# Routed mixture-of-experts layer: second products in half precision, the normalisation split over two engines, and a deep ring of sorted rows

## What is computed

```python
xn = layernorm(x)
# attention part: one gathered number for each token, then a broadcast product
off = xn @ W_off + b_off; w = softmax(xn @ W_attn + b_attn)
s = sum(take(xn[:, 0, :], int(off[..., 0])) * w)
attn = broadcast(s) @ W_out + b_out
# two shared experts, all tokens; eight routed experts, two of them for each token
ffn(x, w1, w2, w3) = silu(x @ w1.T) * (x @ w3.T) @ w2.T     # 128 -> 256 -> 128
shared = sum(ffn(xn, sw1[i], sw2[i], sw3[i]) for i in range(2))
rw, sel = top_k(xn @ router_w.T + expert_bias, 2); rw = softmax(rw)
out = x + attn + shared + sum(rw[k] * ffn(xn, expert sel[k]) for k in range(2))
```

## Time and profile before

| what | us |
|---|---|
| median of 3 runs | 528.65 |
| lowest and highest | 527.91, 529.05 |
| the profiled execution, its time | 530.35 |
| its span, first to last instruction | 528.4 |
| TensorE busy in the span | 453.4 (86%) |
| VectorE busy | 336.8 (64%) |
| ScalarE busy | 219.6 (42%) |
| GpSimd busy | 241.7 (46%) |

### The profile page before, as it was taken

How to read it: one execution, slowest core, us unless ns; L and a number is a source line. 1 busy time by engine, 2 the same in 40 slices (tenths; PEclk the granted TensorE clock), 3 DMA queues, 4 the chain that set the end, 5 groups by cost and what they waited for, 6 DMA issues and landing times.

```text
span 528.4 us, 15190 instructions
## 1 busy us (share of the span) xinstructions
PE 453.4 (86%) x5200; PEld 382.1 (72%) x5200; DVE 336.8 (64%) x973; ACT 219.6 (42%) x399; POOL 241.7 (46%) x225
## 2 busy tenths in 40 slices
PE   0166676787999999999989999999999999999990
PEld 0155533454667777777779999899998999989990
DVE  4899799989676999999756664333333333333330
ACT  1255741172124555554424444344444444443430
POOL 0134400246745333432000001888888887656563
PEclk9999898899999999999989999999999999999997
DMA  8999400000411111111122332445454444232000
GB/s 242 263 156 167 65 1 1 10 26 27 144 53 37 48 51 48 45 45 40 30 89 97 113 103 77 56 53 65 50 67 48 61 57 56 37 52 37 3 3 0
DMA packets 50684, 34.61 MB, mean 65 GB/s; under 512 B 9408, under 2 KB 44224, under 8 KB 50624
## 3 DMA queue, kind: packets, MB, share of 16 engines
q1 hardware_dynamic: 32048, 23.88, 19.9%
q0 software_dynamic: 15296, 8.53, 12.4%
q10 hardware_dynamic: 3280, 1.36, 1.1%
HBM read 14.87 MB, written 20.69 MB: 67 GB/s over the span
## 4 chain that ended last, share of the span: by engine, by line
PE 70%; DVE 18%; issue 3%; DMA 3%; ACT 2%; ACTq 2%; another core or an unknown queue 1%; POOL 0%; DVEq 0%; POOLq 0%
PE pY L611 17%; PE pAB L591 11%; PE pAB L593 8%; PE pAB L592 8%; PE pY L463 7%; DVE units L889 5%; PE pAB L448 4%; PE pAB L450 4%; PE pAB L449 4%; PE pV L488 3%; PE pV L475 3%; PE pV L574 2%; DVE hbuf L913 2%; ACTq L625 2%; DMA base<-in_x 1%
## 5 line engine op out<-in xcount | busy, mean ns | idle before, releaser
L796 POOL DMA_INDIRECT out_dram<-hot,meta x92 | 142.7, 1551 | 62.2 <-DMA out_dram<-base 18.2
L1157 DVE SCALAR_TENSOR_TENSOR hbuf<-pAB,units 128x512 f32<-128x512 f32 x92 | 63.7, 692 | 120.3 <-PE pAB L593 109.1
L591 PE MATMUL pAB<-xT,wsp 128*128 128x128 f16 x736 | 138.2, 220 | 1.7 <-issue 0.8
L593 PE MATMUL pAB<-xT,wsp 128*128 128x128 f16 x736 | 138.4, 220 | 0.0
L592 PE MATMUL pAB<-xT,wsp 128*128 128x128 f16 x736 | 138.2, 220 | 0.0
L777 POOL DMA_INDIRECT sorted_rows<-rows,slot x64 | 70.1, 1096 | 112.7 <-DVE hbuf L913 56.9
L611 PE MATMUL pY<-wsp,hbuf 128*128 x736 | 104.1, 284 | 2.9 <-issue 2.7
L735 ACT ACTIVATE units<-pAB 128x512 f32<-128x512 f32 x92 | 54.9, 597 | 119.8 <-PE pAB L593 117.6
L611 PEld LDWEIGHTS pY<-wsp,hbuf 128*128 128x128 f32 x736 | 89.8, 191 | 5.5 <-issue 3.3
L689 ACT ACTIVATE units<-pAB 128x512 f32<-128x512 f32 x64 | 38.0, 597 | 114.5 <-PE pAB L450 101.3
L591 PEld LDWEIGHTS pAB<-xT,wsp 128*128 x736 | 71.0, 96 | 13.9 <-issue 3.3
(11 more groups left out here) (136 smaller groups left out, 566.0 us busy)
## 6 DMA issues: line engine op xcount, KB each, us to landing
sorted_rows<-c_pad_row SPq DMA_DIRECT2D x1, 6026.0 KB, 46.7
wraw<-sorted_rows SPq DMA_DIRECT2D x46, 131.0 KB
base<-in_x SPq DMA_DIRECT2D x4, 1024.0 KB, 8.2
out_dram<-base SPq DMA_DIRECT2D x16, 256.0 KB, 2.5
wraw<-in_wall SPq DMA_DIRECT2D x8, 256.0 KB
out_dram<-hot,meta POOLq DMA_INDIRECT x92
sorted_rows<-rows,slot POOLq DMA_INDIRECT x64
wsp<-in_wall SPq DMA_DIRECT2D x8, 128.0 KB
```

Of the source, the lines that this page charges most:

```text
L591: pe.matmul(o, hi, x(0), start=True, stop=False)
L593: mm = pe.matmul(o, lo, x(0), start=False, stop=True)
L796: pool.indirect_dma_start(out_rows, bass.IndirectOffsetOnAxis(ap=meta[:, t % Y_RING, DEST - CW:DEST - CW + 1].bitcast(U32), axis=0), yt[:, ...
L1157: v.scalar_tensor_tensor(hbuf[:, r % 4, :], pAB[:, 2 * (r % 2) + 1, :], 1 / (XS * WS), silu[:, r % 2, :], ALU.mult, ALU.mult).then_inc(d_h ...
```

## The change

1. *Front.* ScalarE normalises three of the four tiles of a block (`activation` with scale and bias) and VectorE the fourth; the fp16 high half moves from ScalarE to VectorE. Statistics and scales come in three parts of 4, 4 and 8 blocks instead of two of 8.
2. *Routed second products.* `w2` is split into fp16 halves like `w1` and `w3` (768 columns of each routed expert instead of 512), which takes away eight loads of `w2` by SP. ScalarE makes the fp16 high half of the hidden values (`r_hi`) and VectorE the low half (`r_lo`). TensorE makes 12 fp16 products for a tile instead of four in fp32, and lies one step further behind (`SECOND` = 5). The weight of a row is divided by `WS` for it.
3. *Registers.* An expert's field is taken by a remainder instead of an `&`, and multiplied by `WCOL` at once.
4. *Ring.* `xr` lies in `rows`, 32 pairs deep; loads run up to 8 pairs ahead (`AHEAD`). `r_meta`, `meta` and its GpSimd copies go. SP no longer waits for the last split of the weights before it loads; TensorE does.

```diff
@@ routed stage, TensorE
-            FIRST, SECOND = 2, 4
+            FIRST, SECOND = 2, 5
-                return nc.s_assert_within((word >> at if at else word) & (2 ** FIELD - 1), 0, E - 1,
+                return nc.s_assert_within((word >> at if at else word) % 2 ** FIELD, 0, E - 1,
-                    pe.lower_val(expert(t, k))
+                    pe.lower_val(expert(t, k) * WCOL)
             def r_second(g, r):
-                pe.wait_ge(d_hf, t + 1)
+                pe.wait_ge(d_lo, t + 1)
...
-                        mm = pe.matmul(o, hbuf[:, r % 4, q], second_weight(t, k, h), start=(h == 0), stop=(h == 1))
-                        ready_second(t + 1, k, h)
+                        hi, lo = (first_weight(t, k, s, W2 + h * P) for s in range(2))
+                        pe.matmul(o, h_hi[:, r % 4, q], hi, start=(h == 0), stop=False)
+                        pe.matmul(o, h_hi[:, r % 4, q], lo, start=False, stop=False)
+                        mm = pe.matmul(o, h_lo[:, r % 4, q], hi, start=False, stop=(h == 1))
+                        ready_first(t + 1, k, W2 + h * P, False)
                     ready_expert(t + FIRST_LEAD, k)
@@ routed stage, ScalarE
+            def r_hi(g, r):
+                t = UNROLL * g + r
+                act.wait_ge(d_hf, t + 1)
+                if t >= 4:
+                    act.wait_ge(d_l2, t - 3)
+                nc.scalar.copy(h_hi[:, r % 4, :], hf[:, r % 2, :]).then_inc(d_hi, 1)
-            pipeline(act, TILES, UNROLL, TILES // UNROLL, [(0, r_xt), (5, r_y_first), (2, r_silu)])
+            pipeline(act, TILES, UNROLL, TILES // UNROLL, [(3, r_hi), (0, r_xt), (6, r_y_first), (2, r_silu)])
@@ routed stage, VectorE
-                if past(t, 4):
-                    dve.wait_ge(d_l2, t - 3)
+                if t >= 2:
+                    dve.wait_ge(d_hi, t - 1)
+            def r_lo(g, r):
+                t = UNROLL * g + r
+                dve.wait_ge(d_hi, t + 1)
+                v.tensor_tensor(h_lo[:, r % 4, :], hf[:, r % 2, :], h_hi[:, r % 4, :], ALU.subtract).then_inc(d_lo, 1)
-            pipeline(dve, TILES, UNROLL, TILES // UNROLL, [(0, r_attention), (5, r_y), (2, r_hf)])
+            pipeline(dve, TILES, UNROLL, TILES // UNROLL, [(0, r_attention), (3, r_lo), (6, r_y), (2, r_hf)])
@@ weights: SP and the split
-            for e in range(NSH, NE):
-                sp.dma_start(second[:, :, e, :], wall[e, :, W2:WCOL].rearrange("p (h c) -> p h c", h=2)).then_inc(w2_ready, 16)
-            sp.wait_ge(w_split, NE)
@@ front, ScalarE
+            def normalise(g, r):
+                for j in range(TPB - 1):
+                    t = TPB * i + j
+                    a = nc.scalar.activation(xs[:, r, j, :], base[:, t, :], ACT.Identity, bias=st[:, 1, t:t + 1],
+                                             scale=st[:, 7, t:t + 1])
@@ front, VectorE
+            def rows_high(g, r):
+                v.tensor_copy(rows16[:, TPB * i:TPB * (i + 1), 0:P], xs[:, r, :, :]).then_inc(rows_hi, 1)
-            pipeline(dve, NB, 4, 4, [(0, normalise), (0, second_half), (0, shared_low), (4, read_projections)])
+            pipeline(dve, NB, 4, 4, [(0, normalise_fourth), (0, later_parts), (0, rows_high), (0, shared_low), (4, read_projections)])
```

More of the change, by code:

```diff
@@ L72 @@
 ROUND = 8
-ROOT_STEP = 6
+PARTS = [(0, 4), (4, 8), (8, 16)]
+PART_OF = [k for k, (lo, hi) in enumerate(PARTS) for _ in range(lo, hi)]
+ROOT_AT = {1: 1, 2: 6}
 ATT = 4
@@ L80 @@
 Y_RING, OUT_SEMS = 32, 8
-SEND_FROM = 26
+X_RING, AHEAD = NT // 2, 8
+SEND_FROM = 24
 def constants():
@@ L194, in layer_kernel @@
         units = sb("units", [P, 4, 512], F32)
-        silu = units[:, 0:2, :]
+        silu, hf = units[:, 0:2, :], units[:, 2:4, :]
         xs = units[:].rearrange("p r (j c) -> p r j c", j=TPB)
@@ L320, in layer_kernel @@
         attn_added = sem("attn_added")
-        d_in = [sem(f"d_in{r}") for r in range(RING)]
+        d_in = [sem(f"d_in{r}") for r in range(AHEAD)]
         d_turn = sem("d_turn")
-        d_meta = sem("d_meta")
         d_xt = sem("d_xt")
@@ L655, in turned_copy, with later_roots @@
                 a.then_inc(xt_ready, 1)
-            def second_root(g, r):
-                if 4 * g + r == ROOT_STEP:
-                    root(1)
+            def later_roots(g, r):
+                for k, step in ROOT_AT.items():
+                    if 4 * g + r == step:
+                        root(k)
             def shared_high(g, r):
@@ L807, in _ @@
                     sent += 1
-                if step < TILES and step % 2 == 0:
-                    r_meta(step)
             for t in range(TILES - OUT_SEMS, TILES):
@@ L825, in split_low @@
             def split_low(g, r):
-                row = lambda a: a[:, bass.ds(2 * g + r, 1), 0:W2].rearrange("p o c -> p (o c)")
+                n = W2 if isinstance(g, int) and g == 0 else WCOL
+                row = lambda a: a[:, bass.ds(2 * g + r, 1), 0:n].rearrange("p o c -> p (o c)")
                 dve.wait_ge(w_split_hi, 2 * g + r + 1)
-                v.scalar_tensor_tensor(row(wlo), wraw[:, r, 0:W2], WS, row(whi), ALU.mult, ALU.subtract).then_inc(w_split, 1)
+                v.scalar_tensor_tensor(row(wlo), wraw[:, r, 0:n], WS, row(whi), ALU.mult, ALU.subtract).then_inc(w_split, 1)
             def block_statistics(i):
@@ L836, in block_statistics, with variances @@
                 ins.then_inc(stats_done, 1)
-            def variances(half):
-                part = slice(NT // 2 * half, NT // 2 * (half + 1))
-                dve.wait_ge(stats_done, NB // 2 * (half + 1))
+            def variances(k):
+                part = slice(TPB * PARTS[k][0], TPB * PARTS[k][1])
+                dve.wait_ge(stats_done, PARTS[k][1])
                 of = lambda k: stats[:, part, k]
@@ L848, in variances, with scales @@
                 then(v.tensor_scalar(st[:, 0, part], st[:, 0, part], 0.5, None, ALU.mult))
-            def scales(half):
-                row = lambda k: st[:, k, NT // 2 * half:NT // 2 * (half + 1)]
-                dve.wait_ge(root_ready, half + 1)
+            def scales(part):
+                row = lambda k: st[:, k, TPB * PARTS[part][0]:TPB * PARTS[part][1]]
+                dve.wait_ge(root_ready, part + 1)
                 then(v.reciprocal(row(6), row(5)))
@@ L858, in scales @@
                 then(v.tensor_scalar(row(7), row(7), 2 * XS, None, ALU.mult))
-            for i in range(NB // 2):
+                v.scalar_tensor_tensor(row(1), row(0), -1.0, row(7), ALU.mult, ALU.mult).then_inc(scaled, 1)
+            for i in range(*PARTS[0]):
                 block_statistics(i)
```

126 lines of the change are left out of this document (63 added, 63 removed).

## The result

| kernel | median, us | lowest and highest | ratio to before, 95% interval |
|---|---|---|---|
| before (4 runs beside it) | 528.85 | 527.91, 529.82 | |
| changed (4 runs) | 532.57 | 532.47, 533.43 | 1.0074 [1.0052, 1.0095] |

The change makes the kernel 3.7 us slower. The forecast was 520.0 and a gain: wrong in sign, and outside its range.

A forecast was written before the change was run, and what follows sets the result against it. TensorE was taken to bound the routed stage, then loops between engines at 2.50 us a tile. Routed -7.5, front -2.5 and split +0.5 sum to -9.5: 519.15 us, stated as 520, range 510 to 532.

The forecast's parts named there:

- So TensorE sets the pace: Routed stage before the change: TensorE is the bound at 2.62 us a tile; VectorE and ScalarE follow.
- The gaps behind the plain register instructions, two of 0.07 in a tile, should go: Routed stage, TensorE: two gaps of 0.07 us a tile behind plain register instructions were to vanish.
- 0.82 in place of 0.95: Routed second products on TensorE: 12 fp16 products with two fused register instructions take 0.82 us a tile instead of 0.95.
- 4.76, or 2.38 a tile: Routed stage: TensorE's second products wait for y of two tiles before; that round takes 4.76 us for two tiles.
- Tile with a turned copy 2.64, without 2.16: Routed loop between ScalarE and VectorE, through product, cast, y and silu: 2.64 us with a turned copy, 2.16 without.
- One step more +2.5 and later y +1.0: Routed stage: the pipeline one step longer adds 2.5 us, the last y behind a low half 1.0 us.
- Front -2.5: Front: normalising moved to ScalarE and the cast to VectorE save a net 2.5 us; bounds +1.5 and -5.
- Split, w2 loads, ring, sends: Splits add 0.5 us (bounds 0 and +2.7); w2 loads and ring 0; sends do not bind at 2.50 a tile.
- the second: Rival: routed loops longer than counted; hand-overs of 0.12 us make 2.68 a tile and 536 us; 12 in 100.
- The third: Rival: TensorE stays the routed bound, loops overlap better, 2.33 to 2.40 us a tile, 508 to 513; 12 in 100.
- The first: Rival: VectorE's low half waits for GpSimd's sends in the routed stage, +27 us, so 547; 3 in 100.
- The fourth: Rival: front cast on VectorE goes at one element a cycle, or late blocks wait: +1.5 us, 524; 15 in 100.

The follow-up runs named there:

- regs: The kernel before with only the expert's field taken by remainder and multiplied by `WCOL` at once: 509.08 us, ratio 0.9582 to before.
- more_regs: fp32_second with two more fused register instructions in each tile, their values used by nothing: 517.19 us, ratio 0.9756 to before.
- fp32_second: The changed kernel without the fp16 halves, second products in fp32 as before; new front, fields and ring kept: 505.33 us, ratio 0.9518 to before.
- y_three: The changed kernel with three PSUM banks for y instead of two, the turns keeping one: 526.53 us, ratio 0.9913 to before.
- static_second: y_three with one fixed `w2`, without four fused register instructions a tile (output not the layer's): 512.01 us, ratio 0.9651 to before.
- static_xt_last: static_second with ScalarE's turned copy moved to the end of its step: 518.15 us, ratio 0.9778 to before.

## Why the prediction was wrong, step by step

- **"So TensorE sets the pace": right, for the wrong part of it.** I took 2.62 for the array's. The starts that I had added give 0.95 + 1.33 + 0.11 = 2.39, which is what regs then took (2.40 between loads). The 0.23 left over was the sequencer's, and I had explained 0.14 of it. This is where it failed first.
- **"The gaps behind the plain register instructions, two of 0.07 in a tile, should go": mis-sized, and its worth not followed.** They were worth 0.234 a step. I never asked what this part does without the others, and so no rival held 22 us.
- **"0.82 in place of 0.95": mis-sized, and the step that turned the sign.** From the first second product to the first product it measured 1.06. I had counted 0.074 for an instruction between groups. Two in a row cost 0.13 in mid-tile (0.19 less 0.055) and 0.25 ahead of the first products, where a wait of 0.05 for a semaphore stands behind them. Among fp32 products six such instructions lengthen the stretch far less: in more_regs it takes 1.00 at the median of some 70 tiles, against 0.95 with four of them in fp32_second. Among fp16 products, whose starts alone are 0.67, it takes 1.08. In the round over two tiles the 0.24 make 0.12 a tile, 11 us, more than the whole gain of the forecast. TensorE's whole part was forecast at 2.28. With the round open it was 2.60 between loads and 2.624 with them (y_three).
- **"4.76, or 2.38 a tile" for TensorE's round: mis-sized.** It was 5.28: +0.24 in the second products, +0.14 where y waits for the first half behind the turned copy, which I had left out of this round, +0.11 between y and the second products, where the hand-over was 0.14 and not 0.04, and +0.04 at the product. So the tiles took 2.67 between loads where the sum had 2.50: 0.17 x 92 = 15.6 us. With the front's 1.5 more than forecast, 520 becomes 534, against 532.6 measured. My own sign of being wrong, second products over 2.62 apart, was there.
- **"Tile with a turned copy 2.64, without 2.16": right.** 2.68 in the changed kernel, and 2.453 on average in static_second, which makes 2.23 for the other. It was not what ended last in the mean.
- **One step more +2.5 and later y +1.0: right.** Together 3.5; it was 3.2 from the last product to the last send.
- **Front -2.5: mis-sized, within its bounds.** Front and ring gave 4.0. The first routing instruction starts at 62.3 instead of 66.6, and 3.9 of it is left at the first product. The cast on VectorE took 0.43 at the median, a little over the 0.33 to 0.40 I took and well under 0.61.
- **Split, w2 loads, ring, sends: nothing speaks against them.** VectorE's busy time in the shared stage rose by 1.0 us, and the low half took 0.692 at the median. No run takes one of these parts by itself.
- **Rivals.** The one that came true in sign is the second, slower because loops are longer; its place was for the most part wrong (between ScalarE and VectorE the hand-overs of the tile shown are 0.03, 0.03, 0.04 and 0.10, and 0.14 to TensorE; the register instructions carry most of it). The third had the place, TensorE's own queue, and the wrong size: 2.33 to 2.40 a tile, because it priced that queue as I had. The first fell: the low half does not wait for sends, it was 0.757 at its longest. The fourth fell, by the cast of 0.43, and the fifth, by the clock of 1.00 in the routed stage.

The 29 us of the halves split by the runs as follows. TensorE's own queue, y_three less fp32_second: (2.624 - 2.421) x 91 = 18.5. Two more register instructions alone give 0.145 x 91 = 13.2 of it (more_regs); the other 5.3 come with products that are shorter and eight more in a tile, and no run separates them further. The round over two tiles, changed less y_three: (2.700 - 2.624) x 91 = 6.9. The longer pipeline at the end, 8.7 against 495.1 - 489.5 = 5.6: 3.1. Together 28.5, and 27.9 with a first product that came 0.6 earlier, which is the difference of the two spans (531.6 and 503.7).

## What to carry to other kernels

When short products follow each other, read the weight loads' share and the starts from one product to the next, and subtract: what the array's own spacing and the waits for other engines do not explain is the sequencer's. Count register instructions, since the lengths of their records did not tell the price here. If addresses come from registers, each register instruction in a tile has a price there, about 0.06 to 0.10 us here (0.234 for four plain ones, 0.145 for two fused, 0.390 for four fused), and a change that makes more and shorter products pays it in the open. Of a change with several parts, cost each alone before the sum: here the smallest edit was worth 22 us by itself and the largest one cost 29.

## What the hardware showed that I had not expected

- A plain register instruction is far dearer than its 0.036 us: four fewer in a tile gave 0.234 a step, though the fused ones that were left grew by as much as they had taken. Two fused ones more cost 0.145, though the records of a tile grew by 0.05.
- VectorE's low half, both inputs in SBUF, lengthens a send that starts while it runs. In static_xt_last it had run for 0.18 when the send began, and the send took 1.93; in the changed kernel, one that began 0.5 behind the start of a low half took 1.63. A send that had begun first stayed at 1.55, and so did the low half at 0.69. It is so in all eight kernels with a low half: 158 sends began 0.05 to 0.55 behind the start of one, and in each the offset and the length of the send add up to 2.11 to 2.15, so they end a fixed time after the low half began, wherever they began themselves. No other send is over 1.60, in these kernels or in the six without a low half. The Trainium skill (SBUF — State Buffer, Who interferes with whom) says that a VectorE instruction with two inputs in SBUF contends with a GpSimd instruction that reads SBUF, and that the order of issue decides who blocks. The forecast used this page for a low half that waits; what the rows show is the send that waits, and only for what is left of the low half. In the other order, with the send first, neither grew by more than 0.03, and a low half that waits for the end of a send is in no trace here. No run took the low half away alone, so this rests on the timing of the rows.
